# Three cross-attentions of a fused decoder: eight-head units with natural head rows in place of four-head units with padded rows

## The reference

```
xn = layernorm(x)
q, k, v = heads(xn Wq), heads(ctx Wk), heads(ctx Wv)      # L0x: relu on each, no biases
s = 8 ** -0.5 * q k^T                                     # 16 heads x 128 x 128 for each sequence
L1x: s = where(mask[b], s, -1e9)
x = x + softmax(s) v [Wo + bo]                            # L0x has no Wo
```

## Time and profile before

| | |
|---|---|
| median of three runs | 2350.75 us (2346.02 to 2359.13) |
| profiled execution | 2347.53 us |
| its span, first to last instruction | 2345.5 us |
| granted TensorE clock, mean over the span | 0.848 |
| TensorE matmuls busy | 1660.7 us, 71% of the span |
| VectorE busy | 1427.9 us, 61% |
| ScalarE busy | 879.8 us, 38% |
| GpSimd busy | 91.5 us, 4% |

### The profile page before, as it was taken

The page is one execution under the profiler, slowest core; times in us unless marked ns, Lnnn a source line. Parts: engine busy times, 40 slices in busy tenths (PEclk is TensorE's granted clock), DMA queues, the critical chain, the costliest instruction groups (busy, mean ns, idle before and its releaser), DMA issues.

```text
span 2345.5 us, 29947 instructions
## 1 busy us (share of the span) xinstructions
PE 1660.7 (71%) x9244; PEld 1220.6 (52%) x9244; DVE 1427.9 (61%) x4030; ACT 879.8 (38%) x1409; POOL 91.5 (4%) x82
## 2 busy tenths in 40 slices
PE   5988989997368888869995369899988880000366
PEld 4876876664237557646663247656666440000244
DVE  4544445667865655647776864556657536999445
ACT  4455354563333443434443432255544331010022
POOL 1000000001000000010000100000000000000001
PEclk9999999998679999989996675999989995555568
DMA  2000003000000000000000000000000012000100
GB/s 97 1 0 0 0 1 128 5 4 1 0 0 1 0 0 0 0 14 5 4 5 1 0 0 0 0 5 9 0 1 0 15 29 73 1 1 1 45 9 18
DMA packets 19262, 27.92 MB, mean 12 GB/s; under 512 B 3184, under 2 KB 14320, under 8 KB 18288
## 3 DMA queue, kind: packets, MB, share of 16 engines
q1 hardware_dynamic: 19184, 27.02, 3.4%
HBM read 21.51 MB, written 5.51 MB: 12 GB/s over the span
## 4 chain that ended last, share of the span: by engine, by line
issue 59%; PE 22%; DVE 13%; DVEq 2%; ACT 1%; POOL 1%; DMA 1%; SPq 0%; POOLq 0%; ACTq 0%
PE PSA L550 3%; PE PSA L579 3%; PE PSA L883 2%; PE PSA L559 2%; PE PSA L802 2%; DVE W L1736 2%; DVE W L1725 2%; DVE BIG L1729 1%; PE PSA L819 1%; DVE BIG L1732 1%; PE PSA L622 1%; PE PSA L856 1%; PE PSA L846 1%; PE PSA L778 1%; DVE W L1710 1%
## 5 line engine op out<-in xcount | busy, mean ns | idle before, releaser
L1268 DVE TENSOR_REDUCE MX<-PSA 128x4 f32<-128x512 f32 x320 | 220.9, 690 | 273.2 <-PE PSA L550 129.6
L579 PEld LDWEIGHTS PSA<-VE,PR 128*128 128x128 f32 x2048 | 252.7, 193 | 25.1 <-issue 17.1
L579 PE MATMUL PSA<-VE,PR 128*128 128x9 f32 x2048 | 258.4, 254 | 0.1
L999 ACT ACTIVATE TMP<-TMP 128x512 f32<-128x512 f32 x160 | 100.8, 630 | 338.6 <-DVE TMP L1280 338.6
L550 PE MATMUL PSA<-BIG,QK 128*128 128x512 f32 x384 | 202.2, 615 | 11.1 <-DVE QK L1352 11.1
L910 PE MATMUL PSA<-W,TMP 128*128 128x128 f32 x32 | 8.3, 441 | 263.5 <-DVE TMP L1761 263.5
L1008 ACT ACTIVATE PR<-PSA 128x512 f32<-128x512 f32 x320 | 186.5, 583 | 7.2 <-PE PSA L559 6.6
L999 ACT ACTIVATE PQ<-PQ 128x512 f32<-128x512 f32 x160 | 100.7, 629 | 179.4 <-DVE PQ L1280 179.4
L910 PEld LDWEIGHTS PSA<-W,TMP 128*128 128x128 f32 x32 | 7.1, 327 | 264.6 <-DVE TMP L1761 264.6
L559 PE MATMUL PSA<-K,TMP 128*128 128x128 f32 x640 | 100.5, 279 | 33.0 <-ACT TMP L999 32.2
L559 PEld LDWEIGHTS PSA<-K,TMP 128*128 128x128 f32 x640 | 71.5, 140 | 100.5 <-ACT TMP L999 97.3
(11 more groups left out here) (309 smaller groups left out, 3436.4 us busy)
## 6 DMA issues: line engine op xcount, KB each, us to landing
CTX<-in_ctx_t SPq DMA_DIRECT2D x16, 256.0 KB, 3.1
W<-in_w SPq DMA_DIRECT2D x1, 2048.0 KB, 7.3
ROWS<-in_rows SPq DMA_DIRECT2D x1, 1744.0 KB, 12.2
W<-in_w SPq DMA_DIRECT2D x2, 768.0 KB, 9.4
W<-in_w SPq DMA_DIRECT2D x1, 1412.0 KB, 14.3
W<-in_w SPq DMA_DIRECT2D x2, 640.0 KB, 10.0
W<-in_w SPq DMA_DIRECT2D x2, 512.0 KB, 12.5
scratch_q<-BIG SPq DMA_DIRECT2D x4, 256.0 KB, 2.4
```

The source lines that it names most:

```text
L579: mm = pe.matmul(dst, PR[:, u % 2, tok(j)], val, start=True, stop=True)
L999: act.activation(PQ[u % 2], PQ[u % 2], ACT.Exp, scale=scale).then_inc(exp_ready.sem, 1)
L1268: dve.tensor_reduce(MX[:, tok(u % 4, 4)], tile(PS[1 + u % 3]), AX_X, ALU.max).then_inc(max_taken.sem, 1)
```

## The change

L0x, L1x and L2x leave `small` and get a `cross_attention` of their own on every engine, without a loop: all 32 units of a phase stand one behind another.

- **Head rows.** Weights for q, k and v are 128 by 128, not padded; each projection is one matmul of 512 columns. QN and KN hold heads in their natural rows, 8 to a head, so four heads share 32 rows. GpSimd makes KM from KN, four times over: copy r keeps only the rows of each strip's r-th head (multiplication with the column `lane`). A score matmul takes 32 rows of QN and of KM: it gives the four heads of that strip, 512 columns.
- **Units.** A unit is eight heads, eight units a group: two score matmuls into two banks, one reduction and one subtraction of 1024 columns, one exponential of 1024, eight transposes into two banks, two copies, sixteen product records. Scores run two units ahead.
- **Order.** Projections and transposes for the next group, and outputs of the last one, stand between units and all use bank 7, each after waiting for the one before to be read.
- **Mask.** MASK1 has its own place, is loaded at the start and converted whole during L0a. During L0x a matmul spreads, for each group, whether a query row has any key (SOME); L1x multiplies its queries with it, so that a fully masked row has equal scores. The multiply of the maximum, the matmul with ones and the two fix-up instructions are gone.
- **Zeroing** of BIG for L1x moves to L1f (for L2a, which still uses it).

```diff
-SMALL = ("L0a", "L0x", "L1x", "L2x")
+SMALL = ("L0a",)
+CROSS3 = ("L0x", "L1x", "L2x")
+HALVES = 8
...
-    ("L1x", [("q", 512), ("k", 512), ("v", 128), ("o", 128)]),
+    ("L1x", [("q", 128), ("k", 128), ("v", 128), ("o", 128)]),
...
+        KM = BIG[:, 2048:6144].rearrange("p (n i r t) -> p n i r t", n=2, i=GB, r=4)
+        PH = BIG[:, 6144:8192].rearrange("p (n t) -> p n t", n=2)
...
@@ sync
+                    sp.dma_start(MASK1[:], mask1.rearrange("b o q k -> q (b o) k")).then_inc(masks_loaded, 16)
             for p in run:
-                if p == "L1x":
-
-                    if run[0] != p:
-                        sp.wait_ge(x_updated.sem, x_updated.before[p])
-                    sp.dma_start(MASK1, mask1.rearrange("b o q k -> q (b o) k")).then_inc(masks_loaded, 16)
@@ gpsimd
-            pool.memset(VE[:], 1.0)
+            pool.memset(VE2[:], 1.0)
             pool.memset(ONES[:], 1.0)
+            pool.memset(ONESB[:], 1.0)
...
+            def masked_keys(p, new):
+
+                pool.wait_ge(k_ready.sem, k_ready.at(p, new))
+                for r in range(4):
+                    ins = pool.tensor_scalar(KM[:, new % 2, :, r, :], tile(KN[:, new % 2, :]), col("lane", r), None, ALU.mult)
+                ins.then_inc(km_ready.sem, 1)
...
-                if p in ("L0f", "L1x") and p != run[0]:
+                if p in ("L0f", "L1f") and p != run[0]:
...
+                if p in CROSS3:
+                    ln_root(p, 0)
+                    for new in range(GROUPS):
+                        masked_keys(p, new)
+                        if new:
+                            ln_root(p, new)
+                    continue
@@ tensor
+                def scores(m):
+                    it, e = m // HALVES, m % HALVES
+                    i, h = e // 2, e % 2
+                    if e == 0:
+                        pe.wait_ge(q_ready.sem, q_ready.at(p, it))
+                        pe.wait_ge(km_ready.sem, km_ready.at(p, it))
+                    if m >= 2:
+                        pe.wait_ge(shifted.sem, shifted.at(p, 0, m - 2))
+                    banks = [PS[2 * (m % 2) + n] for n in range(2)]
+                    if p == "L1x":
+                        for n in range(2):
+                            pe.matmul(tile(banks[n]), NEGI[:], mid(MKB[:, it * GB + i, :]), start=True, stop=False, skip_group_check=True)
+                    for n in range(2):
+                        r = strip_of(2 * h + n)
+                        mm = pe.matmul(banks[n], QN[r, it % 2, tok(i)], KM[r, it % 2, i].rearrange("p r t -> p (r t)"),
+                                       start=p != "L1x", stop=True, skip_group_check=True)
+                    mm.then_inc(s1_psum.sem, 1)
+
+                def transposes(m):
+                    pe.wait_ge(exp_ready.sem, exp_ready.at(p, 0, m))
+                    for c in range(2):
+                        if m:
+                            pe.wait_ge(p_ready.sem, p_ready.at(p, 0, 2 * (m - 1) + c))
+                        for j in range(4):
+                            mm = pe.transpose(PS[4 + c][:, tok(j)], PH[:, m % 2, tok(4 * c + j)], ident)
+                        mm.then_inc(t_psum.sem, 1)
...
+                scores(0)
+                scores(1)
+                transposes(0)
+                for m in range(GROUPS * HALVES):
+                    it, e = m // HALVES, m % HALVES
+                    if m + 2 < GROUPS * HALVES:
+                        scores(m + 2)
+                    if m + 1 < GROUPS * HALVES:
+                        transposes(m + 1)
+                    product(m)
+                    more = it + 1 < GROUPS
+                    if e == 0 and more:
+                        project_keys(it + 1, misc())
+                        freed = k_ready, k_ready.at(p, it + 1)
...
+                    if e == 1 and it and p != "L0x":
+                        freed = outputs(it - 1)
+                    if e == 2 and it and p != "L0x":
+                        freed = project(it - 1)
+                    if e == 3 and more:
+                        project_queries(it + 1, misc())
+                        freed = q_ready, q_ready.at(p, it + 1)
...
+                    if e == 5 and more:
+                        project_values(it + 1, misc())
+                        freed = v_ready, v_ready.at(p, it + 1)
+                    if e == 7 and more:
+                        next_xnt(it + 1, misc())
+                        freed = xnt_ready, xnt_ready.at(p, it + 1)
@@ scalar
+                exp(0)
+                for m in range(GROUPS * HALVES):
+                    if m + 1 < GROUPS * HALVES:
+                        exp(m + 1)
+                    copies(m)
+                    if m:
+                        after(m - 1)
@@ vector
+                if p == "L1x":
+                    dve.wait_ge(some_ready.sem, some_ready.at("L0x", GROUPS - 1))
+                    queries(0, PS[5])
+                values(0, PS[6])
+                next_moments(p, 0)
+                for u in range(GROUPS * HALVES):
+                    it, e = u // HALVES, u % HALVES
+                    softmax_inputs(u)
+                    if u == 0:
+                        next_normed(p, 0)
+                    if e == 0 and it:
+                        values(it, PS[7])
+                    if u >= 3 and u % 2:
+                        normalise(u // 2 - 1)
...
+                    if e == 5 and it and p != "L0x":
+                        update(it - 1)
+                    if e == 5 and p == "L1x" and it + 1 < GROUPS:
+                        queries(it + 1, PS[7])
+                    if e == 5 and it + 1 < GROUPS:
+                        next_moments(p, it + 1)
+                    if e == 7 and it + 1 < GROUPS:
+                        next_normed(p, it + 1)
```

More of the change, by code:

```diff
@@ L391, in kd_zeroed @@
         def kd_zeroed(p):
-            return sum(q in run[1:run.index(p) + 1] for q in ("L0f", "L1x"))
+            return sum(q in run[1:run.index(p) + 1] for q in ("L0f", "L1f"))
         def strip_of(j):
@@ L546, in scores1 @@
                                        start=True, stop=True)
[L547 to L551, removed]
                 mm.then_inc(s1_psum.sem, 1)
@@ L993, in xnt_next, with exponentials @@
                 act.wait_ge(xnt_psum.sem, xnt_psum.at(p, it))
-                act.activation(XNT[:], PS[XNT_BANK.get(p, 2)], ACT.Copy).then_inc(xnt_ready.sem, 1)
-            def exponentials(p, it, scale, fill=None):
+                act.activation(XNT[:], PS[7 if p in CROSS3 and it is not BEFORE_LOOP else XNT_BANK.get(p, 2)], ACT.Copy).then_inc(xnt_ready.sem, 1)
+            def exponentials(p, it, scale):
                 def exp(u):
@@ L1012, in exponentials @@
                         xnt_next(p, it)
-                    if u == UNITS - 2 and fill:
-                        fill()
                 if p == "L1a":
@@ L1190, in _ @@
                         scan(it)
-                if p in ("L1a", "L1x") and kd_zeroed(p):
+                if p in ("L1a", "L2a") and kd_zeroed(p):
                     act.wait_ge(kd_zero, kd_zeroed(p))
-                if p == "L0x" or p in ("L0a", "L2a", "L2x"):
+                if p == "L0a":
                     act.wait_ge(setup_pool, 1)
@@ L1201, in _ @@
                     for g in range(HG):
-                        keys(p, 0, g, range(3))
+                        keys(p, 0, g)
                     with act.Fori(0, GROUPS - 1) as it:
@@ L1373, in first_keys @@
-                def first_keys():
-                    keys(p, it + 1, 0)
-                    keys(p, it + 1, 1)
-                attend(p, it, normalise, fill=first_keys if more else None)
-                if p == "L0x":
-                    dve.drain()
-                    add_to_x(p, it, ON[:])
+                dve.drain()
+                for j in range(2, 4):
+                    for ins in spread_q(dve.tensor_copy, j):
+                        pass
+                    ins.then_inc(qd_ready.sem, 1)
@@ L1837, in _ @@
                     continue
+                if p in CROSS3:
+                    cross_attention(p)
+                    continue
                 if p in SMALL:
-                    if kd_zeroed(p):
-                        dve.wait_ge(kd_zero, kd_zeroed(p))
-                    for g in range(HG):
-                        keys(p, 0, g)
                     values(p, 0)
@@ L1900, in lay_out @@
     parts = {}
-    for p, t in (("L0a", "L0_attn"), ("L0x", "L0_xattn"), ("L1x", "L1_xattn")):
-        parts[f"{p}.q"] = strips(a[f"{t}_Wq"].T)
-        parts[f"{p}.k"] = strips(a[f"{t}_Wk"].T)
-        parts[f"{p}.v"] = a[f"{t}_Wv"].T
+    parts["L0a.q"], parts["L0a.k"], parts["L0a.v"] = strips(a["L0_attn_Wq"].T), strips(a["L0_attn_Wk"].T), a["L0_attn_Wv"].T
+    for n in "qkv":
+        parts[f"L0x.{n}"], parts[f"L1x.{n}"], parts[f"L2x.{n}"] = a[f"L0_xattn_W{n}"].T, a[f"L1_xattn_W{n}"].T, a[f"L2_xattn_W{n}"]
     parts["L0a.o"] = a["L0_attn_Wp"].T
@@ L1938, in lay_out @@
         for n in "qk":
```

(7 more changed lines are left out.)

398 lines of the change are left out of this document (249 added, 149 removed), and 4 rows, old and new, of the table W_PARTS.

## The result

The changed kernel took **2515.16 us** (median of 4 runs, 2514.29 to 2545.67) against 2348.48 for the kernel before on the same chip; the ratio is 1.073, 95% interval 1.065 to 1.082. The forecast was 2262, with a range from 2220 to 2306, and faster. It was wrong: the change made the kernel slower.

The account below looks back on a forecast made before the run. TensorE was taken to bound the three changed phases; gains of 24.4 us in L0x, 40.4 in L1x and 20.8 in L2x, less 0.6 of setup, came to -85 from 2347.5, so 2262 us, range 2220 to 2306.

Parts of the forecast that it names:

- Part 1: Eight-head unit of the changed phases, costed from TensorE's earlier durations: 4.5 us a unit in L0x and L2x, 4.85 in L1x.
- Rival D: Changed phases: granted clock falls to 1.2 GHz from pauses or quarter-full arrays, TensorE's 4.4 us becomes 8.8; 2660 us, 5%.
- B: Rival: score matmuls on two strips overlap, unit 4.25 us (4.6 in L1x), 23 us less; 2239 us, 22%.
- Masked copies: GpSimd's four masked key copies ahead of a phase's first scores: 0.7 us each, 2.8 for four.
- The start of L1x: Start follows VectorE, free at 1027.4 us; units begin at 1034.5, where in the kernel before they begin at 1043.7.
- The last two units: End of each changed phase: 30 steps at the usual unit time, then 1.8 us for the last product alone.
- The zeroing moved to L1f: GpSimd's zeroing of BIG in L1f: 6.9 us, hidden before its first root there with 3 us to spare.
- VectorE's and ScalarE's widths: Softmax of a unit: 1.22 us for 1024 columns on VectorE, exponential 1.16; 2.5 and 2.3 us a unit.
- the group boundary that goes: Between groups: 12 to 15 us now; work slipped between units still costs TensorE 13.8 us a phase, 10.6 in L0x.
- TensorE's waits: L1x and L2x: at unit e = 3, 1.9 us in two groups; at e = 5, 2 to 3 us a phase.
- Rival E: Group boundary stays, as each bank-7 handover costs a full pause: 55 us more, 2317 us, 6%.
- rival C: Change-overs between whole-array and strip matmuls exposed, two a unit: unit 4.9 us, 37 us more; 2299 us, 17%.

## Why the prediction was wrong

**The step that failed** is the clock under the unit. Part 1 took TensorE's durations from the earlier trace rows, at 0.99, and kept them for a unit whose scores read 32 rows. "The 32 rows instead of 128 shorten nothing" was right for the streaming of one matmul, and wrong for the clock: rows fell from 128 to 32 and the clock of L0x from 1.00 to 0.50. Rival D named the mechanism, the granted clock, and its sentence on "arrays a quarter full" the cause; it got 5%. The evidence I set against it, L1x's pauses at 0.95, spoke of pauses, not of rows, and no row of before had a matmul with fewer rows than 128. A resource that no row shows needed a wide chance, not 5%.

**D's size, 2660, was off** because B was true as well. At the lower clock, 8.7 us a unit was the price without overlap; the run with one strip has that (2727). Side by side, scores take 2.0 instead of 3.7. Between the two profiled executions lie 225 us. L0x and L2x have 53 each, which is 31 steps of 1.7. L1x has 90, because its clock is lower with one strip too (0.54 against 0.64 over the phase). Another 26 lie between L1x and L2x, where neither edit reaches, at a clock of 0.64 against 0.72. I treated B and D as alternatives, and they come together from the same edit.

**The rule on overlap** (the Trainium skill, TensorE: Matmul & The Clock Gate, Part 3: matmuls on different row groups run concurrently) agrees with the trace: four instructions on two strips in 1.06 us, eight on four strips in 2.09 at the lower clock. The rule that a change of tiling mode drains the engine (the Trainium skill, TensorEngine Tiling, Key Properties) fits the 0.2 us left at one of the two changes; I had bounded both together by 0.5. The remark of the Trainium skill on transposes (TensorE: Matmul & The Clock Gate, Part 4) decides nothing here: transposes stayed, only rows changed.

**With the clock restored, the sum is 29 us short.** The run to hold against 2262 is the one with masked queries, 2291, whose GpSimd order is that of the forecast. Its unit is no longer than the forecast 4.5: 4.30 (472.23 to 476.53) or 4.43. Five terms were too small:
- Masked copies took 1.56 us each, not 0.7: 3.4 us at each start. The bound, less than the root's 1.01, came from another kind of instruction and was no bound.
- The start of L1x. TensorE waits for the last update of X before its first projection (idle 6.73 us ahead of it), so first scores come 14.2 us after that update in the changed kernel, not 7.2: 3.6 for the projections, which I had as done by then, and the rest is the copies.
- The last two units have no scores, and their clock falls: 32 product records took 6.83 us in L0x in the 128-row run, twice the 3.4 of the full clock. I had forecast a fast end.
- The zeroing moved to L1f was not free. VectorE's three multiplies of the weights now run beside it, and slower:

```profile
1352.95 6.92 POOL L510 MEMSET BIG<- 128x8192 f32 x1 [76.79 <-DVE X L1438]
1357.95 2.99 DVE L1702 TENSOR_SCALAR BIG<-W,WSC 128x512 f32<-128x512 f32 x3
```

```profile
1269.24 1.28 DVE L1489 TENSOR_SCALAR BIG<-W,WSC 128x512 f32<-128x512 f32 x3
```

The last row is of the kernel before, so it cost 1.7 us. In L0f, where both kernels zero BIG at this place, they take 2.99 in both. I had looked only at GpSimd's own queue.
- What stands behind L2x takes 620 to 622 us in every version of the changed kernel, 615 before, and I had put it at nothing. The first group of L2f starts at the lower clock and is 3 us longer in the version with keys first; the rest I did not trace.

In the run with masked queries the three phases are 7, 8 and 6 us longer than forecast, counted from the first projection, in L1x from the last update; some 5 lie behind L2x and 2.5 between L0x and L1x. In the 128-row run L0x gained 16, L1x 31 (from L0x's last product) and L2x 12, where 24, 40 and 21 were forecast, 26 less in all; with L1f's and L2a's slower clock (12.9 us, 285.3 against 272.4) and 6 behind L2x this makes up about the 43 us by which it misses 2262. The version with keys first, at 2270.55, lies only 8 us above the 2262, but that is luck: its order on GpSimd, which the forecast kernel did not have, gives back 4 to 5 us at each start.

**Right:** VectorE's and ScalarE's widths (1.225 us for 1024 columns against 1.22; the exponential 1.06 against 1.16), the group boundary that goes, CTX for L1x already there, and TensorE's waits: 2.08 us at e = 3 in two groups of L1x and L2x (1.9 forecast), none at e = 5. Rival E doesn't appear. Of rival C, 0.2 us shows at one of the two changes of a unit.

## What to carry to other kernels

Take a change of how many rows matmuls read as a change of TensorE's clock until a run shows otherwise: before costing a unit from rows at 2.4 GHz, ask whether its main matmuls still look the same to the array. If a contraction is short, zero rows in a masked copy of the small operand can be cheaper than a strip: four copies a group on ScalarE bought back 224 us (2515 to 2291). And look at the first instruction behind each moved one on every engine, as the root ahead of the masked keys cost 4 to 5 us in each phase for no reason.

## What the runs showed of the hardware that I had not expected

- Granted clock by the rows of the score matmuls, all else equal (L0x of the kernel before, mean over 160 us): 1.00 with 128, 0.92 with 96, 0.56 with 64, 0.59 with 32; in the changed kernel 0.97 with 128, 0.50 with 64 and with 32, while TensorE was busy for 99% of the stretch. Rows of zeros count as rows (0.98 with masked queries).
- Matmuls on different strips overlap also as float32 pairs: 2.01 us on two strips against 3.71 on one, at 1.2 GHz.
- A GpSimd multiply of 128x512 float32 by a column took 1.56 us, a cast to bf16 of the same size 0.61.
- Three VectorE multiplies between SBUF tensors took 2.99 us beside a GpSimd memset and 1.28 without one.
